# Softmax divided behind the value product, layer-norm columns as values, an unrolled slot order

## The reference

```
e0, e1 = E0[tokens], E1[tokens]
p = stack(e0 @ W0 + b0, e1 @ W1 + b1)        # two projections, 64 wide
h = sum(p * softmax(p @ Wa + ba), over the two)
x = layernorm(h)
q, k = x @ Q[h], x @ K[h]                    # 8 heads, 32 wide
attn = softmax(q @ k.T / 8)                  # 512 x 512 for each head
h = h + sum over heads of (attn @ x) @ VO[h] # VO is 64 x 64
y = layernorm(h)
H = gelu(y @ W1 + b1)                        # 256 wide
probs = softmax(H @ Wg + bg)                 # 8 experts, the best one is used
h = h + probs[best] * (H @ Wd[best] + bd[best])
```

## Time and profile before

| | us |
|---|---|
| median of 3 runs (541.0 to 550.81) | 544.9 |
| the profiled execution's span | 541.9 |
| TensorE matmuls busy | 461.3 |
| VectorE busy | 413.8 |
| ScalarE busy | 353.5 |
| GpSimd busy | 162.3 |

### The profile page before, as it was taken

The page is one execution under the profiler, slowest core; times in us unless marked ns, Lnnn a source line. Parts: engine busy times, 40 slices in busy tenths (PEclk is TensorE's granted clock), DMA queues, the critical chain, the costliest instruction groups (busy, mean ns, idle before and its releaser), DMA issues. The chain is left out here.

```text
span 541.9 us, 8152 instructions
## 1 busy us (share of the span) xinstructions
PE 461.3 (85%) x1792; PEld 221.9 (41%) x1792; DVE 413.8 (76%) x853; ACT 353.5 (65%) x833; POOL 162.3 (30%) x270
## 2 busy tenths in 40 slices
PE   0358699998999899988999899989999899989474
PEld 0134254344544454444544454445444444333151
DVE  4558987889789988989799888998899766621335
ACT  0006587887976698668868687669767987863220
POOL 3040130014028400751056203740182017204404
PEclk9995579999999999999999899999999999989858
DMA  5023332323222312232222312232222222000000
GB/s 136 0 56 90 82 80 68 84 61 82 60 61 59 81 46 66 51 85 59 59 58 52 84 45 58 69 81 54 64 53 67 51 70 58 20 2 1 10 0 10
DMA packets 23918, 30.73 MB, mean 57 GB/s; under 512 B 8847, under 2 KB 10458, under 8 KB 23898
## 3 DMA queue, kind: packets, MB, share of 16 engines
q1 hardware_dynamic: 22362, 28.05, 20.5%
q0 software_dynamic: 1536, 2.46, 2.0%
HBM read 4.00 MB, written 1.05 MB: 9 GB/s over the span
## 5 line engine op out<-in xcount | busy, mean ns | idle before, releaser
L396 ACT ACTIVATE prob<-st_ps 128x512 f32<-128x512 f32 x256 | 153.2, 601 | 82.9 <-PE st_ps L816 70.7
L389 ACT ACTIVATE s_ps<-s_ps,neg_max 128x512 f32<-128x512 f32 x256 | 170.3, 665 | 46.6 <-DVE neg_max L468 43.4
L468 DVE TENSOR_REDUCE neg_max<-s_ps 128x1 f32<-128x512 f32 x256 | 172.2, 682 | 24.5 <-PE s_ps L807 24.1
L828 PE MATMUL ctx_ps<-prob,val 128*64 128x512 f32 x512 | 140.5, 628 | 0.0
L816 PE MATMUL st_ps<-qst,kst 98*128 98x512 f32 x256 | 133.1, 522 | 0.7 <-ACT prob L396 0.6
L807 PE MATMUL s_ps<-kst,qst 96*128 96x512 f32 x256 | 110.4, 438 | 9.5 <-ACT s_ps L389 5.0
L349 POOL COPY val<-raw_v 128x256 f32<-128x256 f32 x64 | 25.5, 403 | 167.4 <-PE ctx_ps L828 152.5
L899 PE MATMUL sh_ps<-wd,hid 128*128 128x512 f32 x128 | 70.5, 642 | 2.9 <-DVE yb L673 2.6
L816 PEld LDWEIGHTS st_ps<-qst,kst 98*128 98x128 f32 x256 | 49.2, 194 | 49.8 <-issue 32.5
L807 PEld LDWEIGHTS s_ps<-kst,qst 96*128 96x128 f32 x256 | 51.3, 201 | 37.9 <-ACT s_ps L389 16.5
L329 POOL TENSOR_TENSOR yc<-yb,coef 128x512 f32<-128x512 f32 x30 | 32.1, 1069 | 76.8 <-DVE yb L673 47.7
(11 more groups left out here) (92 smaller groups left out, 509.7 us busy)
## 6 DMA issues: line engine op xcount, KB each, us to landing
qst<-raw_q SPq DMA_DIRECT2D x192, 64.0 KB, 2.0
kst<-raw_k SPq DMA_DIRECT2D x192, 64.0 KB, 2.0
...
rows<-emb,idx POOLq DMA_INDIRECT x32
...
qst<-shift_t SPq DMA_DIRECT2D x32, 8.0 KB
...
```

What stands on the lines that cost most here:

```text
L389: nc.scalar.activation(ps[:, :], ps[:, :], ACT.Exp, bias=neg_max[:, n:n + 1], scale=-1.0, accum_out=den[:, n:n + 1]).then_inc(s_exp, 1)
L396: nc.scalar.activation(prob[:, n % P_BUFS, :], st_ps[n % ST_BANKS][:, :], ACT.Exp, scale=-1.0).then_inc(p_done, 1)
L468: V.tensor_reduce(neg_max[:, n:n + 1], s_ps[n % S_BANKS][:, :], AX.X, ALU.min).then_inc(max_done, 1)
L828: last = PE.matmul(ctx_ps[d * C:(d + 1) * C, :], val[:, h, c + d, :], prob[:, (2 * pair + d) % P_BUFS, :], start=(pair == 0), stop=(pair = ...
```

## The change

The softmax is no longer finished before the value product.

- `exp_scores`, the sums and the logarithm are gone. The shift is the row's extreme alone, made for a pair of heads (`shift_parts`, `PT` = 8 tiles) and not for four.
- The values are the layer norm's own columns: `xa` holds 63 of the 64 columns of x and a column of ones, for all heads. Its product with the unnormalised probabilities gives attn @ x times the sum, and the sum itself. Since a layer-norm row sums to zero, the missing column is put in the weights: `vox` holds VO minus its last row, and a column that picks the sum. The projections of the values, their copies, and `store_v` are gone.
- `context` accumulates per pair of heads, each head in its half of `ctx_ps`. `ctx_out` copies the bank four times a sequence; `project_out` multiplies it with `vox` (130 columns, plain f32, eight slots `vo00` to `vo31` a sequence); `normalise_heads` divides by the sum on VectorE; `accumulate_heads` adds the heads on GpSimd. The transposes of the context are gone.
- Copies out of PSUM of the embedding, x, the high halves of q and k, the shift and the context move from VectorE to ScalarE; gelu reads PSUM itself; products with the embedding's weights and its mix move to GpSimd.
- Two score banks in place of three, three shared banks in place of two. A score bank is free once the maximum is taken.
- `LEAD` is 17, the tables are new, nothing is looped. Several tiles (`ctx_s`, `h1`, `res`, `coef`, `rows`) are doubled.

```diff
-LEAD = NT - 8
-S_BANKS, ST_BANKS, SH_BANKS = 3, 2, 2
+LEAD = 17
+S_BANKS, ST_BANKS, SH_BANKS = 2, 2, 3
 WHEN_T = {
+    "e0_t": -50, "e1_t": -48, "proj": -44, "proj_t": -42, "x_t": -26, "q0": -23, "k0": -22, "q1": -15, "k1": -14,
...
 WHEN_V = {
+    "k1": -12, "parts": -9, "norm0": 14, "norm1": 16, "layer1": 43, "normal1": 47, "gate": 58, "tops": 58,
...
+WHEN_S = {"stack": -20, "shift": -6, "out": 71}
+STACK_STEP = 3
...
-        def exp_scores(act, b, n):
-            at_least(act, max_done, NT * b + n + 1)
-            nc.scalar.activation(ps[:, :], ps[:, :], ACT.Exp, bias=neg_max[:, n:n + 1], scale=-1.0,
-                                 accum_out=den[:, n:n + 1]).then_inc(s_exp, 1)
...
+        def accumulate_heads(pool, b, p):
+            GP.tensor_tensor(zsum[:, :, :], zp[:, :, 0, :], zp[:, :, 1, :], ALU.add).then_inc(zsum_ready, 1)
+            GP.tensor_tensor(h1[b % 2][:, :, :], before, zsum[:, :, :], ALU.add).then_inc(acc_done, 1)
...
+        def normalise_heads(dve, b, p, u):
+            V.reciprocal(own, ps[:, :, 2 * C:2 * C + 2]).then_inc(rden_ready, 1)
+            V.tensor_tensor(z[p % 2][:, 2 * u:2 * u + 2, :, :], ps[:, :, 0:2 * C].rearrange("p c (h e) -> p c h e", e=C),
+                            own.unsqueeze(3).to_broadcast([P, 2, 2, C]), ALU.mult).then_inc(emptied[name], 1)
...
-                last = PE.matmul(ctx_ps[d * C:(d + 1) * C, :], val[:, h, c + d, :], prob[:, (2 * pair + d) % P_BUFS, :],
-                                 start=(pair == 0), stop=(pair == NT // 2 - 1))
+                last = PE.matmul(ctx_ps[d * C:(d + 1) * C, :], xa[b % 2][:, c, :], prob[:, (2 * m + d) % P_BUFS, :],
+                                 start=(c == 0), stop=(c == J - 1))
...
+        def project_out(pe, b, p, u):
+            claim(pe, name, b)
+            pe.wait_ge(ctx_read, PAIRS * b + p + 1)
+            for c in range(2):
+                last = PE.matmul(bank(name, b)[:, c * VOW:(c + 1) * VOW], ctx_s[p % 2][:, q:q + P], vox[:, p, :], start=True, stop=True)
```

More of the change, by code:

```diff
@@ L292, in lm_tower @@
-        EMB_ALL, W_ALL, LATE_ALL = 16 * 3, 16 * 2, 16 * 4
+            for s in range(FIRST, LAST):
+                for h in range(H):
+                    for b in due(s, WHEN_S["stack"] + STACK_STEP * h):
+                        stack_head(sp, b, h)
+                for p in range(PAIRS):
+                    for b in due(s, WHEN_S["shift"] + PT * p):
+                        store_shift(sp, b, p)
+                for b in due(s, WHEN_S["out"]):
+                    store_out(sp, b)
+            for n in range(2):
+                sp.wait_ge(out_stored[n], 16 * (B // 2))
@@ new lines, in split_high, with row_out @@
+        def split_high(act, b, g, which):
+            name = f"{which}{g}"
+            raw, scale = (raw_q, -1.0 / C ** 0.5) if which == "q" else (raw_k, 1.0)
+            act.wait_ge(filled[name], b + 1)
+            for h in range(g * HG, (g + 1) * HG):
+                at_least(act, stacked[h], STACK * b)
+            AC.activation(raw[g][:, 0, :], bank(name, b)[:, :], ACT.Copy, scale=scale).then_inc(high_ready[name], 1)
+        def row_out(act, b, p):
+            act.wait_ge(filled[f"row{p}"], b + 1)
+            if p >= 2:
+                act.wait_ge(shift_stored[p - 2], 32 * (b + 1))
+            else:
+                at_least(act, shift_stored[p + 2], 32 * b)
+            AC.activation(shift_t[p % 2][:, :], bank(f"row{p}", b)[0:2 * PT, 0:P], ACT.Copy).then_inc(emptied[f"row{p}"], 1)
@@ L834, in transposes, with embed_t @@
             for j, piece in enumerate(pieces):
[L835 removed]
+                last = PE.transpose(bank(name, b)[0:rows_, j * P:(j + 1) * P], piece, ident[:, :])
             last.then_inc(filled[name], 1)
[L838 removed]
+        def embed_t(pe, b, n):
             if n == 0:
[L840 to L841 removed]
@@ L843, in embed_proj @@
-        def embed_proj(pe, i, b):
-            claim(pe, i, "proj")
+                pe.wait_ge(rows_loaded, 16 * J * (b + 1))
+            transposes(pe, f"e{n}_t", b, [rows[b % 2][:, j, n * EMB:(n + 1) * EMB] for j in range(J)], EMB)
+        def embed_proj(pe, b):
+            claim(pe, "proj", b)
             for n in range(2):
-                at_least(pe, emptied[f"e{n}_t"], b + 2)
-                last = PE.matmul(bank("proj")[n * C:(n + 1) * C, :], emb_w[:, n, :], rows_t[:, n, :], start=True, stop=True)
+                pe.wait_ge(emptied[f"e{n}_t"], b + 1)
+                last = PE.matmul(bank("proj", b)[n * C:(n + 1) * C, :], emb_w[:, n, :], rows_t[:, n, :], start=True, stop=True)
```

965 lines of the change are left out of this document (445 added, 520 removed), and 12 rows, old and new, of tables (WHEN_T, WHEN_V).

## The result

The changed kernel takes 578.6 us (median of 4 runs, 575.9 to 584.1) against 543.0 us before, measured beside it (540.7 to 550.8): a ratio of 1.069 with a 95% interval of 1.062 to 1.076. It is slower by more than 2%. The ratio leaves out the slow execution of 550.8 us, which lies more than 1.5% above the fastest of its kernel. 553 us was forecast; 578.6 lies 6.6 us above the top of the range.

What follows compares the result with a forecast made beforehand. It took the order of TensorE's work with its waits as the bound. Prologue 57.1 + stage 0 49.8 + 5 x 60.0 + stage 6 57.3 + stage 7 45.5 + tail 40.2 = 549.9 us span, plus 3.0: 553 us, range 530 to 572.

Steps and rivals of the forecast that it cites:

- the stack: Slot 15: TensorE waits for six DMAs of the next sequence's head 0; 3.0 us, from 2.3 to 3.6.
- raw_q: Slot 19: hid0 takes q1's bank and waits for VectorE's low half of q1; 1.5 us.
- raw_k: Slot after hid0: the embedding product waits likewise for k1; 0.3 us.
- yb: Slot 1: y3 takes y2's bank, whose copy is last in VectorE's slot 0; 0.8 us.
- proj: Slot 22: transposes of proj wait for a ScalarE copy behind the gelu block; 0.5 us.
- SyncE's queue: Prologue: first shift issues behind five heads' stacks on SyncE; first L816 at 57.1 us, 13.0 us earlier.
- the wait for SyncE at slot 8: Stage 0: SyncE still stacking heads, so slots 0 to 7 last 12.8 us, not 10.5; 24 more slots take 33.6.
- TensorE's own work: Full stage: 52.1 us before, 53.6 after, bounds 53.2 to 56.8; waits before taken as 5.6 us.
- The eight product slots: Full stage: two 130-column f32 products in each slot, 0.50 us a slot, adding 4.0 us.
- rival (c): Full stages: wait for head 0's DMAs lowers TensorE's clock, 1.7 us lost in each of six stages, 563 us; chance 0.37.
- ScalarE's relief at nothing: Score tiles: removing 256 exponentials, at least 154 us of ScalarE, costed at nothing, hidden behind TensorE's work.
- Unrolling at nothing: Full stages: writing out the sequence loop costed at nothing, with other bound -2.0 us a stage.

Runs made afterwards that it cites:

- e2: Changed kernel with 12 extra 512-column matmuls on TensorE ahead of the wait for head 0's stack; 564.9 us, 1.045 times before.
- e9: Changed kernel reordered: heads 0 and 1 stacked earlier, embedding's product beside gelu one sequence ahead, q1 and k1 earlier, y3 later; 532.9 us, 0.981 times before.
- e6: Changed kernel with one idle 512-column exponential on ScalarE ahead of each slot's own, 256 in all; 594.9 us, 1.102 times before.
- e7: Kernel before the change with its loop over sequences 1 to 5 written out, nothing else; 538.0 us, 0.992 times before.

## Why the prediction was right or wrong

**The direction and the places: right.** The growth of a full stage, its waits for the stack, raw_q, raw_k, yb and proj, each at the slot named, and the earlier start were all found.

**The start and the tail: right. Stages 0 and 7: right in size, by luck.** The start took 58.4 for 57.1: SyncE's queue was the right step, with 19.0 us from the first issue to that of the first shift rows (36.78 to 55.77), as forecast, begun 1.5 later. In the tail (41.1 for 40.2) the mean starts 11.7 us after the last L735, for 11.6. Stage 0 came out at 51.0 for 49.8. Its terms in the prediction (12.8, 33.6 and a wait of 3.0) add up to 49.4; it lost 8.5 us to the clock, which was not in the sum, and the wait for SyncE at slot 8, which was, is not in the trace. TensorE ran at half its clock until 72.0 and was at slot 8 only at 71.87; in e2, where the clock was back at 65.8, it waits there 1.97 us. Stage 7 came out at 45.5 for 45.5, but with a wait for prob of 2.04 us that I did not have, 0.24 for y3 where I had 1.1, and 43.0 of own work where I had 44.4.

**TensorE's own work: right sum, wrong parts.** I had 52.1 before and 53.6 after. Busy time at full clock says 53.6 before and 55.6 - 1.7 = 53.9 after; it grew by 0.3, not 1.5. The base was 1.5 too low (so the waits of before were 3.9 a stage and not 5.6). The eight product slots at 0.36 add 2.9, not the 4.0 I took; with 2.9 the prediction's own list gives a growth of 0.4.

**The waits: near, a little low.** In the stage from 298.73, by its own trace: stack 3.45 for 3.0, raw_q before hid0 1.38 for 1.5, raw_k 0.37 for 0.3, yb before y3 1.16 for 0.8, proj_t 0.47 for 0.5. One was not foreseen: x2_t takes the bank of the embedding's transposes and waits 0.61. Together 7.4 for 6.4. The stack's wait reached 4.0 in another stage, past my bound of 3.6. Its step held: two rows of the changed kernel in order of time show VectorE's low half and the first issue of the stack.

```profile
320.51 0.68 DVE L556 SCALAR_TENSOR_TENSOR raw_k<-sh_ps,raw_k 128x512 fp32r<-128x512 f32 x1
...
321.25 1.81 SPq L200 DMA_DIRECT2D qst<-raw_q  x3
```

From the first issue to the reader, the score matmul at 326.43 shown above, 5.18 us pass, against the 5.26 of the earlier trace rows. The Trainium skill, "DMA: Bandwidth & Descriptors", section "Anatomy of one DMA", counts some 2 us of fixed cost for one DMA on the path of GpSimd. For one of SyncE's, the page of the profile has the same figure (2.0 us from issue to landing), but six issued in a row by one queue stand before the reader, and that decides.

**The step that failed: rival (c) was set beside the forecast and not into it.** I had the price right (1.7 us for a fall of the clock) and the place right, and weighed it at 0.37 because the waits for values of before mostly left the clock at 1.00. But those waits were 1.5 us on average and at most 1.9, and the one I was forecasting was 3.0. No wait of that length stood in the stages I had read, so their full clock was no evidence against the fall. It came in all seven stages that have the wait, and in half of stages 1 to 6 it lasted twice as long (3.4 us lost), for which I had no term. The forecast's sum has nothing for the clock; the runs showed 15.4 us in stages 1 to 6. The stage from 298.73 by terms: 53.9 + 7.4 + 1.7 = 63.0, measured 63.2. Over stages 1 to 6 the clock is 15.4 us of the 20.8 by which they exceed the forecast, and e2 shows most of it as a cost on the path. The remaining 5 are waits 7 us larger and own work 1.5 us smaller than forecast. The Trainium skill, "TensorE: Matmul & The Clock Gate", Part 1, has the gate fall after idleness. By that rule, as the prediction took it, every stage with such a wait would pay, and the trace of the changed kernel agrees: all seven do. The four falls of e9 at no wait are not told by it.

**The range failed with it.** It ended at 572 on a stage of 62; 63.4 was measured.

**ScalarE's relief at nothing: wrong** by 16 us in this order (e6), with two stages in which the clock, not the waits, was the greater part. **Unrolling at nothing: wrong** by 3 us within its bound (e7). Neither error shows in the forecast's miss: the sum went by TensorE's work and waits, which contain them.

**What stays open.** Why the clock's loss is 1.7 us in some stages and 3.4 in others (in the changed kernel it was 3.4 where the low clock began 0.24 to 0.43 us before TensorE resumed, and 1.7 where it began within 0.1 us of that or later); what makes the clock fall in e9; and what the gaps are, too short for the listing, by which TensorE's time differs between orders.
